# Attention and feed-forward block: another step order, q and k scaled in PSUM, feed-forward weights split earlier, first up products moved among the last tiles

## The reference, cut to what matters

```python
x = x + attn(cond(x, itok_B_0_15))      # x: 128 batches x 32 positions x 512
x = x + ffn(cond2(x, itok_B_3_7))

cond : einsum('bct,bcd->bdt', x, style_w[ids])             # a 32x32 matrix for each batch
attn : qkv = clip(h @ w_qkv.T, -8, 8); q, k = layer_norm(q), layer_norm(k)
       probs = softmax(q @ k.T / 4 + alibi, causal)        # 32 heads of 16, sequence 32
       out = (probs @ v) @ w_out.T
cond2: y = x @ w2[adapter].T                               # a 512x512 matrix for each batch
ffn  : h = relu(y @ up_w) ** 2                             # 512 -> 1024
       routed = (y @ fc1 @ expert @ fc2) * sum(top2(y @ gate))
       out = layer_norm(h @ down_w + routed)
```

## Time and profile before

| | |
|---|---|
| median of 3 runs | 1329.23 us (1325.96 to 1337.59) |
| the profiled execution's own time | 1333.75 us |
| its span, first to last instruction | 1332.0 us |
| PE busy | 1194.6 us, 90% |
| POOL, DVE, ACT busy | 683.6, 657.3, 522.1 us |
| mean granted clock of TensorE | 0.953 of full |
| moved by DMA | 131.39 MB, 99 GB/s |

### The profile page before, as it was taken

One profiled execution on the slowest core, in us unless ns is written; L12 is line 12 of the kernel. 1 busy time (PEld: TensorE's weight loads), 2 busy tenths in 40 slices (PEclk: granted clock), 3 DMA queues, 4 the chain that ended last, 5 costly groups with the idle time before them and its releaser, 6 DMA issues. The chain is left out here.

```text
span 1332.0 us, 27187 instructions
## 1 busy us (share of the span) xinstructions
PE 1194.6 (90%) x11076; PEld 924.6 (69%) x11076; DVE 657.3 (49%) x1020; ACT 522.1 (39%) x863; POOL 683.6 (51%) x676
## 2 busy tenths in 40 slices
PE   7789889988899879898998777999999999999995
PEld 4567667767677657676776444677878787877884
DVE  5356655555557655464657423244434344443433
ACT  4245454555554545555564414313031322213020
POOL 3246766757667668686866433324233333333242
PEclk9789989989998889999998888999999999999998
DMA  6013233243333333433332486502112020200100
GB/s 243 24 43 106 89 111 129 96 126 103 104 128 100 126 103 99 132 106 129 111 126 91 145 309 222 205 24 64 48 48 79 32 79 27 69 32 32 48 24 32
DMA packets 47770, 131.39 MB, mean 99 GB/s; under 512 B 10272, under 2 KB 11040, under 8 KB 41888
## 3 DMA queue, kind: packets, MB, share of 16 engines
q1 hardware_dynamic: 35424, 95.57, 21.9%
q0 software_dynamic: 12224, 34.10, 7.4%
HBM read 87.68 MB, written 27.79 MB: 87 GB/s over the span
## 5 line engine op out<-in xcount | busy, mean ns | idle before, releaser
L521 PE MATMUL bank<-wqkv_hi,h_hi 128*128 128x512 f32 x384 | 164.1, 427 | 0.3
L521 PE MATMUL bank<-wqkv_lo,h_hi 128*128 128x512 f32 x384 | 153.9, 401 | 0.0
L521 PE MATMUL bank<-wqkv_hi,h_lo 128*128 128x512 f32 x384 | 153.8, 400 | 0.0
L1352 POOL TENSOR_TENSOR w_lo<-w2t,w_hi 128x512 fp32r<-128x512 f32 x104 | 136.4, 1342 | 7.1 <-issue 6.4
L1402 POOL TENSOR_TENSOR u_lo<-act,u_hi 128x512 fp32r<-128x512 f32 x64 | 85.9, 1348 | 101.7 <-ACT u_hi L1004 101.7
L1407 POOL TENSOR_SCALAR fve<-fmv 128x1 f32<-128x1 f32 x32 | 25.0, 782 | 200.5 <-DVE fmv L1256 200.5
L1341 POOL TENSOR_TENSOR probs<-probs,row_max 128x1024 f32<-128x1024 f32 x32 | 61.3, 1916 | 106.8 <-DVE row_max L1152 106.7
L1148 DVE SCALAR_TENSOR_TENSOR probs<-pair,cst 128x512 f32<-128x512 f32 x64 | 41.2, 686 | 149.2 <-PE pair L579 149.2
L690 PE MATMUL bank<-yT_hi,up_hi 128*128 128x512 f32 x256 | 103.1, 403 | 0.0
L1017 ACT ACTIVATE ys<-bank,weight 128x512 f32<-128x512 f32 x32 | 22.1, 690 | 203.2 <-PE bank L706 203.2
L713 PE MATMUL pair<-down_hi,u_lo 128*128 128x512 f32 x256 | 101.3, 396 | 0.0
(11 more groups left out here) (183 smaller groups left out, 2993.7 us busy)
## 6 DMA issues: line engine op xcount, KB each, us to landing
w2t<-in_w SPq DMA_DIRECT2D x38, 1024.0 KB
vx<-v_hl SPq DMA_DIRECT2D x128, 68.0 KB
kx<-k_hl SPq DMA_DIRECT2D x128, 64.0 KB, 1.9
x_rows<-x1t SPq DMA_DIRECT2D x32, 256.0 KB
w2t<-x_rows SPq DMA_DIRECT2D x32, 256.0 KB, 3.1
yt<-y_rows SPq DMA_DIRECT2D x4, 1024.0 KB, 6.9
w2t<-y_rows SPq DMA_DIRECT2D x4, 1024.0 KB, 6.8
stage<-in_wqkv SPq DMA_DIRECT2D x3, 1024.0 KB, 9.0
```

Of the source, the lines that this page charges most:

```text
L521: m = e.matmul(into, a[:, c, :], b[:, n, c, :], start=(c == 0 and k == 0), stop=(c == KC - 1 and k == 2))
L1352: e.tensor_tensor(w2_lo[:, c, :], w2t[0][:, c, :], w2_hi[:, c, :].bitcast(F32), ALU.subtract).then_inc(d_wlo, 1)
```

## The change

- **Step order.** `values` and `scores` are written in halves of 48 matmuls, with a projection or the output projection between the halves. q of tile i-1 is turned right behind `turn_values`, then the slot's product, then k is turned. The other engines' lists are reordered to fit. The slot's product goes to bank B2 and B4 is freed for the new work.
- **q and k in PSUM.** `scale_q` and `scale_k` write back to the bank that they read. The high and low parts (`high_q`, `low_q`, `high_k`, `low_k`) are made out of the bank; `qT` and `kT` are gone. The third projection bank is free for the next tile only when `low_k` is done, the second only when `low_q` is.
- **Weights of the feed-forward part.** From step 4 to step 23 one chunk of 128 x 512 (20 in all) is loaded in each step, split (ACT twice: high part, and a copy into B4; DVE: B4 minus high part) and both parts are stored in DRAM. ACT issues eight loads of 2 KB rows for the finished parts from step 31 on.
- **End of the attention.** No drain steps: behind step 31 stands a list written out by hand, in which the last four tiles are finished and `up(0, 0)` to `up(0, 4)` stand among them. All slots are split now; slots 26 to 37 are done two in each of the feed-forward groups 0 to 5, one among the up products, one behind `down(m, 0)`.
- **Buffers.** One `w2t` instead of two, two `act`, `x1g` and `ot` instead of three, four and three; one `yt`. `w2_lo` is made by one POOL instruction of 2048 columns instead of four of 512.

```diff
-            for i in range(STEPS):
+            for i in range(T):
                 live = lambda t: 0 <= t < T
                 slot = i >= LAG
-                drain = i >= T
                 if 0 < i < T - 1:
                     style(i + 1)
                 if live(i):
                     upto(e, "cq", i - 1)
+                    if i > LAG:
+                        e.wait_ge(d_mc, i - LAG)
                     project(i, 0, B2, "pq")
                 if i == 0:
                     make_route(2)
                     style(1)
-                if drain:
-                    turn_slot(i - LAG)
                 if live(i - 4):
-                    values(i - 4)
+                    values(i - 4, 0)
                 if live(i):
                     upto(e, "ck", i - 1)
-                    upto(e, "qT", i - 2)
+                    upto(e, "qhi", i - 2)
+                    upto(e, "qlo", i - 2)
                     project(i, 1, B3, "pk")
                 if i == 0:
                     make_route(3)
                 if live(i - 4):
-                    turn_values(i - 4)
-                if drain:
-                    adapt_slot(i - LAG)
+                    values(i - 4, 1)
+                if slot:
+                    turn_slot(i - LAG, B7)
                 if live(i):
                     if i == 0:
                         e.wait_ge(s_tables, 2)
                     upto(e, "cv", i - 1)
-                    upto(e, "kT", i - 2)
+                    upto(e, "khi", i - 2)
+                    upto(e, "klo", i - 2)
                     project(i, 2, B5, "pv")
-                if slot and not drain:
-                    turn_slot(i - LAG)
+                if live(i - 4):
+                    turn_values(i - 4)
+                if live(i - 1):
+                    upto(e, "ck", i)
+                    turn_qk(i - 1, qn[(i - 1) % 2], "qn", B3, "tq")
+                if slot:
+                    adapt_slot(i - LAG, B2)
+                if live(i - 1):
+                    upto(e, "cv", i)
+                    turn_qk(i - 1, kn[(i - 1) % 2], "kn", B5, "tk")
+                if live(i - 2):
+                    scores(i - 2, 0)
                 if live(i - 4):
                     out_project(i - 4)
-                if live(i - 1):
-                    upto(e, "ck", min(i, T - 1))
-                    turn_qk(i - 1, qn[(i - 1) % 2], "qn", B3, "tq")
-                    upto(e, "cv", min(i, T - 1))
-                    turn_qk(i - 1, kn[(i - 1) % 2], "kn", B5, "tk")
-                if slot and not drain:
-                    adapt_slot(i - LAG)
                 if live(i - 2):
-                    scores(i - 2)
-
-
-            for s in range(TAIL, SLOTS):
-                k = s - TAIL
-                if k < 2:
-                    turn_slot(s)
-                if k and s + 1 < SLOTS:
-                    turn_slot(s + 1)
-                adapt_slot(s)
-                if k == 0:
-                    for c in range(KC):
-                        turn(0, c)
-                if k == 2:
-                    gate_products(0)
-                if k == 3:
-                    turn_gates(0)
+                    scores(i - 2, 1)
...
+
+            e.wait_ge(d_mc, LAST + 1)
+            turn_qk(T - 1, kn[(T - 1) % 2], "kn", B2, "tk")
+            turn_qk(T - 1, qn[(T - 1) % 2], "qn", B7, "tq")
+            upto(e, "khi", T - 2)
+            upto(e, "klo", T - 2)
+            turn(0, 0)
+            upto(e, "qhi", T - 2)
+            upto(e, "qlo", T - 2)
+            turn(0, 1)
+            values(T - 4, 0)
+            values(T - 4, 1)
+            turn(0, 2)
+            turn(0, 3)
+            scores(T - 2, 0)
+            scores(T - 2, 1)
+            turn_values(T - 4)
+            up(0, 0)
+            out_project(T - 4)
+            values(T - 3, 0)
+            values(T - 3, 1)
+            up(0, 1)
+            turn_values(T - 3)
+            scores(T - 1, 0)
...
+            def high_chunk(n):
+                e.wait_ge(r_raw, 16 * (n + 1))
+                e.activation(w_high[:, :], w_raw[:, :], ACT.Copy).then_inc(r_high, 1)
+                upto(e, "olo", n)
+                e.activation(B4, w_raw[:, :], ACT.Copy).then_inc(r_bank, 1)
...
-            def scale_q(t):
+            def scale_q(t, at):
                 upto(e, "tq", t)
-                upto(e, "qlo", t - 1)
                 for c in range(KC):
-                    m = e.activation(qT[:, c, :], B3[:, P * c:P * c + P], ACT.Identity,
+                    m = e.activation(at[:, P * c:P * c + P], at[:, P * c:P * c + P], ACT.Identity,
                                      bias=qkln[:, KC + c:KC + c + 1], scale=qkln[:, c:c + 1])
...
+            def high_q(t, at):
+                upto(e, "qT", t)
+                upto(e, "s", t - 1)
+                e.activation(q_hi[:, :, :], at.rearrange("p (c t) -> p c t", c=KC), ACT.Copy) \
+                    .then_inc(A["qhi"], 1)
...
+            def low_k(t, at, dst):
+                upto(e, "khi", t)
+                if t < T - 1:
+                    upto(e, "kx", t - 1)
+                e.tensor_tensor(dst[:, 1, :], at, dst[:, 0, :], ALU.subtract).then_inc(A["klo"], 1)
...
+                if i == T - 1:
+                    e.wait_ge(r_kept, 32 * CHUNKS)
+                    upto(e, "pq", T - 1)
+                    fetch(m_up, up_hi[:, 0:4, :], 0, 0, 4)
+                    fetch(m_up, up_lo[:, 0:4, :], 1, 0, 4)
```

More of the change, by code:

```diff
@@ L120, in program @@
     route_rows = nc.dram_tensor("route_rows", [P, KC, DM], F32, kind="Internal").ap()
+    ffn_parts = [nc.dram_tensor(f"ffn_{n}", [CHUNKS, P, DM], F32, kind="Internal").ap() for n in ("high", "low")]
     top = ExitStack()
@@ new lines, in adapt_slot @@
+                e.wait_ge(d_tl, s + 1)
+                e.wait_ge(d_whi, s + 1)
+                e.wait_ge(d_wlo, s + 1)
+                if s <= LAST:
+                    upto(e, "cq", min(s + LAG, T - 1))
+                    if s:
+                        e.wait_ge(d_mc, s)
+                for c in range(KC):
+                    for k, (a, b) in enumerate(((xgT_hi, w2_hi), (xgT_hi, w2_lo), (xgT_lo, w2_hi))):
+                        m = e.matmul(into, a[:, P * c:P * c + P], b[:, c, :], start=(c == 0 and k == 0),
+                                     stop=(c == KC - 1 and k == 2))
@@ L1209, in _ @@
[L1209 to L1220 removed]
+                upto(e, "pk", t)
@@ new lines, in _ @@
+            low_o(T - 4)
+            bias_max(T - 2)
+            low_q(T - 1, B7)
+            square(0)
+            add_x(T - 4)
+            divide(T - 3)
+            turn_probs(T - 2)
+            low_o(T - 3)
+            square(1)
+            bias_max(T - 1)
+            square(2)
+            add_x(T - 3)
+            turn_probs(T - 1)
+            divide(T - 2)
+            low_o(T - 2)
+            square(3)
+            divide(T - 1)
+            add_x(T - 2)
+            low_o(T - 1)
@@ new lines, in low_w2, with low_probs @@
+            def low_w2(s):
+                e.wait_ge(d_whi, s + 1)
+                e.tensor_tensor(w2_lo[:, :, :], w2t[:, :, :], w2_hi[:, :, :].bitcast(F32),
+                                ALU.subtract).then_inc(d_wlo, 1)
+            def low_probs(t):
+                upto(e, "phi", t)
+                upto(e, "o", t - 1)
+                e.tensor_tensor(p_lo[:, :], probsT[:, :], p_hi[:, :], ALU.subtract).then_inc(A["plo"], 1)
+            for i in range(T):
+                live = lambda t: 0 <= t < T
+                t = i
+                if live(i + 2):
+                    style(i + 2)
```

1068 lines of the change are left out of this document (583 added, 485 removed).

## The result

The median is 1193.4 us over 4 runs (1191.27 to 1193.86), against 1327.7 us for the kernel before (4 runs, 1325.96 to 1337.59). The ratio is 0.8987 with a 95% interval of 0.893 to 0.9045: 10% faster, near the 1190 predicted. The profiled execution took 1193.86 us for a span of 1192.1.

A forecast was written before the change was run, and what follows sets the result against it. PE was taken as the bound, losing 113 us in steady attention to stops, k's low part and low clock. Terms 117.5 + 470 + 39 + 47 + 502.5 + 15.5 gave a 1191.5 us span, forecast 1190 us, range 1160 to 1236.

The forecast's parts named there:

- Halves: Steady attention steps: four runs of 48 small matmuls instead of two of 96 remove nearly all PE stops, -50 us.
- rival 4: Stops come with something else in the same place, as the w2 load; halves keep them, 1240 us; chance 0.07.
- The price of a split: Two more changes between small and long matmuls per step cost perhaps 0.3 us, 7 us in all.
- q and k in PSUM: Attention steps: low part of k takes 0.65 instead of 5.94 us; 16.5 us wait goes, with most of 28 us low clock.
- POOL next: Steady steps: POOL needs 18.5 to 19.5 us, nearly PE's 19.1, so 19.6 us a step; POOL busy above 85%.
- Rivals 2 and 5: 2: POOL, with ACT, becomes the bound, 1213 us, chance 0.17. 5: w2 lands late every step, 1335 or more, 0.03.
- Chunks: Weight chunks in 20 attention steps cost 0 to 0.5 us a step, inside the 19.6.
- Start: Up to step 6: style matrix first in POOL's step removes waits, -8 us (-3 to -14), 117.5 instead of 125.5.
- End of the attention and feed-forward part: Written-out list replacing drain and slots: 47 us (41 to 56); feed-forward groups with 12 added slots: 502.5 us (496 to 515).
- the 6 us for waits: Feed-forward part: 0.5 us for each of 12 slots, as the slot behind down(m, 0) may wait for w2_lo.
- rival 3: Feed-forward weights arrive late: up(0, 0) or down(0, 0) waits 20 us, 1210 us; chance 0.09.
- my last sign of being wrong: The prediction is wrong if PE waits in the feed-forward part at all.

The follow-up runs named there:

- the joined kernel with the scatter moved: The changed kernel with both halves joined into runs of 96 and POOL's scatter of y_rows moved behind the gathers, ahead of p_lo: 1173.85 us, ratio 0.8936.
- the joined kernel: The changed kernel with the halves of values and scores put together again into runs of 96, all else kept: 1190.57 us, ratio 0.9022.
- the changed kernel with its scatter moved: The changed kernel, halves kept, with POOL's scatter of y_rows moved behind the two gathers: 1199.6 us, ratio 0.9123.
- quarters: The changed kernel with the scores in four runs of 24, three parts of the output projection between them: 1189.23 us, ratio 0.9006.
- the single edit: The kernel before with only POOL's style matrix of tile i+2 made first in its step instead of last: 1297.47 us, ratio 0.9779.
- the kernel with the late up products: The changed kernel with up(0, 0) to up(0, 4) put behind the last tiles on all engines: 1204.71 us, ratio 0.9176.

## Why the prediction was right, and where it was wrong

**The sum held because its errors cancelled.** By stage, measured and predicted:

| | predicted | measured |
|---|---|---|
| to step 6 | 117.5 | 106.75 |
| 24 steady steps | 470 | 481.9 |
| steps 30 and 31 | 39 | 38.4 |
| written-out list | 47 | 51.4 |
| feed-forward part | 502.5 | 498.1 |
| end | 15.5 | 15.5 |
| span | 1191.5 | 1192.1 |

(The feed-forward part is counted here to the end of the last product, 1176.6 us, 2.1 us behind the cut in the stage view above.) I had the start 10.8 us too long and the feed-forward part 4.4, the steady steps 11.9 too short and the list 4.4. That they meet within a microsecond is luck.

**Halves: the step that failed.** "The stops begin at 41 or later, so nearly all should go: -50 us." Of 77 stops 26 are left, but the halves earned nothing by it. Without them the changed kernel has 41 stops, not 77, and the same time (1190.6 and 1193.4); alone in the kernel before they bring the stops down to 26 as well, but PE waits elsewhere instead. What took most of the stops away in the changed kernel is POOL's order: in the earlier trace rows its gathers stand at the end of the step, under the scores; after, they stand at 499 to 501.4, ahead of p_lo, where PE does long products. Moving them so in the kernel before removed all stops in the scores (57 to 0); moving the style matrix, which shifts the gathers, left 4 of 77 in all. This is the prediction's rival 4, "something else that falls in the same place", with another something than its w2 load, and with its consequence turned round: the reordering moved that thing as well.

The rule of the Trainium skill that the prediction weighed (Runtime: NRT & Kernel Launch, "Instruction fetch mechanics": prefetch is hidden) did better than I gave it credit for where the scores are concerned: 28 of 29 such runs of 96 pass without a stop in the joined kernel with the scatter moved. The trace agrees with it there. It doesn't in `values`, where ten stops of the same kernel, 0.2 to 1.5 us each, follow the start of an instruction transfer by 2.2 to 2.5 us: here the measurement decides. No run here shows by what path an indirect transfer of POOL keeps PE waiting.

**The price of a split was too low.** I put two splits at 0.3 us a step. A step of the joined kernel without a stop takes 18.75 us; the changed kernel's, 19.84 with one stop that shows 0.57 us, should be 19.27 without it, and the two steps without a stop of the changed kernel with its scatter moved take 19.33 and 19.37: 0.5 to 0.6 us for two splits. The quarters agree: two splits more, no stop, 19.8. So a split costs some 0.26 to 0.3 us, 13 to 15 us for two in 26 steps, and the halves saved 15 stops of 0.65 us, 10 us. This and the stop left in each step are why a step took 20.08 instead of 19.6.

**q and k in PSUM: right, and larger.** The low part of k takes 0.68 us, the wait is gone, the clock is back at 1.00. Alone it gives 48 us (1327.8 to 1279.3), close to 16.5 + 28. With the rule of the Trainium skill that the prediction named (SBUF — State Buffer, "SBUF: two separate sides") the trace agrees: the low part of k takes 0.68 us at most, and another subtraction with one operand in PSUM, h_lo, takes no more than 0.68 in the 22 times that it stands beside w2_lo. An addition with both inputs in SBUF took up to 4.16 us beside w2_lo in the feed-forward part, and PE didn't wait for it, as predicted. The steady part's 83 us are then 50 stops of 0.73 (37 us), 16.5 of the wait and 28 of the clock (an estimate from its mean), 81.5; the 13 us of small waits that went too about pay for the splits.

**POOL next: wrong.** I saw its list at 18.5 us and took it for nearly the bound. It is 16.7, and POOL waits 3.1 us in each step; it is busy 77% of the steady part and not above 85%. The 1.8 us between are w2_lo (5.48 us in four pieces in that step, 4.62 in one piece now), 0.3 us of the first operation on the variance, and shorter gaps: time that I had counted as fixed work. Rivals 2 and 5 did not come: ACT waits 14.5 us in all 24 steps for the w2 load, POOL 4.9 for ACT, PE for neither.

**Chunks: right.** Steps 6 to 23 take 20.18 us on average and steps 24 to 29, without chunks, 19.79: 0.39 us, inside the 0 to 0.5. Even that is mostly longer stops: in the quarters, which have none, the two figures are 19.86 and 19.85.

**Start: right mechanism, half the size.** The style matrix first is worth 17.9 us there by itself, and I had -8, with -14 as the bound; the change gained 18.8. PE's waits before, between 18 and 126 us, begin with this row:

```profile
PE bank L511 <- issue: 14.2, 6, 5.6
```

It is gone in both kernels that build the matrix first. The wait came back in each of the first three steps (in the single edit they are 5.8, 6.3 and 4.8 us shorter), and I had counted it about once.

**End of the attention and feed-forward part: near.** In the list PE waits 4.7 us for the load of y, 4.4 for four other things, and works at a clock of 0.87: 51.4 for 47. Twelve slots cost 498.1 - (472.3 - 13.8) = 39.6 us, 3.3 each; the 6 us for waits were 1.0, and PE never waited for w2_lo there. No rival 3: nothing waits for the weights. But my last sign of being wrong, any wait of PE in this part, did come, 2.7 us.

## What to carry to other kernels

Where an engine stops for nothing that the profile shows, lay the stops beside every other engine's rows before explaining them by what the engine itself does; the common factor of 335 of 352 stops was an instruction of POOL that the stopped matmuls don't wait for. Then look at those that don't fit: here 14 of 17 had a second cause in common. Measure by starts too, since idle times hide short stops. Place POOL's indirect transfers where PE has long matmuls, and after every move on POOL look where the next transfer lands. Test a part of a change alone on the kernel before: here the halves, which looked essential, were worth nothing, and what looked like a detail of POOL's order took most of the stops away.

## What the runs showed of the hardware

- A run of small matmuls (64 x 32 by 128 columns, or 128 x 32 by 68) stops while POOL executes an indirect transfer of about 1.05 us, in most cases after 41 or more of them: mostly 0.3 to 0.5 us idle, 0.65 to 0.73 us lost, up to four times in a run of 96 that meets two transfers. Of 352 stops in eleven kernels 335 lie at one (the kernel with the late up products, 27 of 28, is not counted). Runs of 24 or 32 had no idle time above 0.15 us. Why the length matters stays open.
- 14 of the other 17 stops end at a matmul whose place among PE's records is 194 above a multiple of 256, 2.2 to 2.5 us after a transfer of 16 KB began on the queue of instructions; the ten in the fastest kernel are 8.8 us idle together. Why these transfers begin late stays open, and no run tested it.
- Changing between small and long matmuls costs PE 0.13 to 0.15 us each time (0.26 to 0.3 for a split), seen in steps without a stop of 18.75 us (no split), 19.33 and 19.37 (two) and 19.8 (four).
- Such small matmuls begin some 8 ns apart when nothing stops them: 88 of 96 within 0.72 us.
- One POOL subtraction of 2048 columns takes 4.62 us; four of 512 took 5.04 and 5.48 in the two steps shown.
